# A decoder layer on one core: values masked by ScalarE, four state products per batch on GpSimd, and a new order of the projection units

## What is computed

```
dA = exp(A * dt);  dBu = dt * Bm * hs          # 1024 channels, 16 states, 256 positions
s_l = dA_l * s_(l-1) + dBu_l                   # the scan
y = sum over n of s[n] * Cm[n]                 # "C product", then the sum over the states
v = Wv @ source + bv;  out = (softmax(mask * q.k ...) * mask) @ v    # masked values
scale = max(mean(|w|), eps);  wq = clip(round(w / scale), -1, 1)     # ternary weights
```

## Time and profile before

| | us |
|---|---|
| median of three runs | 3782.39 (3778.49 to 3785.61) |
| the profiled execution | 3785.51 |
| span of its profile | 3783.6 |
| mean granted TensorE clock | 0.94 |
| state-space steps, first scan to last scan | 87.7 to 2087.3 |

### The profile page before, as it was taken

One profiled execution on the slowest core, in us unless ns is written; L12 is line 12 of the kernel. 1 busy time (PEld: TensorE's weight loads), 2 busy tenths in 40 slices (PEclk: granted clock), 3 DMA queues, 4 the chain that ended last, 5 costly groups with the idle time before them and its releaser, 6 DMA issues. The chain is left out here.

```text
span 3783.6 us, 53475 instructions
## 1 busy us (share of the span) xinstructions
PE 3172.5 (84%) x16161; PEld 1878.1 (50%) x16194; DVE 3054.2 (81%) x2990; ACT 2540.9 (67%) x4872; POOL 2143.7 (57%) x1352
## 2 busy tenths in 40 slices
PE   6878888888888888888876478898898899859998
PEld 4666566656665666566655233343343333324444
DVE  1999998989989989899999377777787777638887
ACT  3878787877777877777776035565565556647777
POOL 1888887878888878788888123343243334210000
PEclk9989999999999999999996789999999999989999
DMA  4012101110121012101110445454553544331111
GB/s 151 3 57 70 71 14 58 70 71 12 59 71 71 12 60 70 69 10 63 71 65 1 123 134 153 137 158 134 161 160 114 171 149 128 102 100 42 44 44 37
DMA packets 157518, 311.41 MB, mean 82 GB/s; under 512 B 21969, under 2 KB 77393, under 8 KB 157089
## 3 DMA queue, kind: packets, MB, share of 16 engines
q1 hardware_dynamic: 152880, 299.46, 24.6%
q10 hardware_dynamic: 4352, 8.39, 0.6%
HBM read 216.11 MB, written 91.69 MB: 81 GB/s over the span
## 5 line engine op out<-in xcount | busy, mean ns | idle before, releaser
L681 DVE TENSOR_TENSOR_SCAN states<-states,bu 128x1024 f32<-128x1024 f32 x512 | 1173.7, 2292 | 188.4 <-POOL bu L612 107.2
L612 POOL TENSOR_TENSOR bu<-du,bc 128x1024 f32<-128x1024 f32 x512 | 1196.3, 2361 | 117.1 <-DVE states L681 113.9
L545 ACT ACTIVATE states<-dt,negA 128x256 f32<-128x256 f32 x2048 | 853.1, 464 | 440.6 <-DVE hc L693 380.4
L1162 ACT ACTIVATE pt<-s_ps 128x512 f32<-128x512 f32 x1024 | 573.4, 597 | 427.9 <-PE s_ps L1057 418.7
L1313 DVE TENSOR_REDUCE mmax<-s_ps 128x2 f32<-128x1024 f32 x512 | 624.4, 1223 | 288.0 <-PE s_ps L1048 272.8
L421 PE MATMUL y_ps<-id_sb,hc 128*128 128x128 f32 x4096 | 575.3, 286 | 143.3 <-DVE hc L693 143.2
L693 DVE TENSOR_TENSOR hc<-states,bc 128x1024 f32<-128x1024 f32 x512 | 626.8, 1224 | 52.3 <-DVE states L681 0.9
L421 PEld LDWEIGHTS y_ps<-id_sb,hc 128*128 128x128 f32 x4096 | 490.8, 147 | 308.1 <-DVE hc L693 262.6
L1057 PE MATMUL s_ps<-qst,kst 105*128 105x512 bf16 x1024 | 387.0, 392 | 13.1 <-ACT pt L1162 5.1
L1048 PE MATMUL s_ps<-kst,qst 102*128 102x512 bf16 x1024 | 325.3, 401 | 83.9 <-issue 42.7
L390 PE MATMUL proj<-xpad,diagW 128*128 128x256 f32 x1024 | 260.4, 388 | 42.1 <-ACT xpad L488 42.1
(11 more groups left out here) (153 smaller groups left out, 4529.3 us busy)
## 6 DMA issues: line engine op xcount, KB each, us to landing
bc<-bc_scratch SPq DMA_DIRECT2D x128, 512.0 KB, 4.7
stack_d<-parts SPq DMA_DIRECT2D x192, 256.0 KB, 3.0
w_raw<-in_w_ffn SPq DMA_DIRECT2D x32, 768.0 KB, 6.1
qst<-stack_d SPq DMA_DIRECT2D x64, 384.0 KB
kst<-stack_d SPq DMA_DIRECT2D x64, 384.0 KB
x<-xres SPq DMA_DIRECT2D x32, 512.0 KB, 3.5
xT_sb<-in_xT SPq DMA_DIRECT2D x16, 512.0 KB, 3.5
xres<-in_x SPq DMA_DIRECT2D x16, 512.0 KB, 3.7
```

The source lines that it names most:

```text
L545: a = act.activation(states[:, bank, first:first + SEQ], dt[:, t, :], ACT.Exp, scale=negA[:, t, c * NS + n:c * NS + n + 1])
L612: pool.tensor_tensor(bu[:, buf, :].rearrange("p (n l) -> p n l", n=NS), du[:, t % (2 * GRP):t % (2 * GRP) + 1, :].to_broadcast([P, NS, SEQ ...
L681: m = dve.tensor_tensor_scan(dst, dst, bu[:, BU_OF[k][0], half * 2 * SEQ:(half + n) * 2 * SEQ], 0.0, ALU.mult, ALU.add)
L1162: act.activation(pt[:, g % 2, u % HG, st, :], s2_ps[:, st % 2], ACT.Exp).then_inc(exp_done, 1)
```

## The change

1. **C products.** At steps 0, 12, 20 and 28 of each batch (`POOL_STEPS`) the scan writes to a new SBUF buffer `hp`, and POOL multiplies it by C three steps later (`times_C` of the gpsimd block, after `inputs` of that step). PE adds it to `y_ps` two steps after its own step. The wait of `decays` two steps on is then for the scan, not for the product.
2. **Order of units.** `LONG`, `SHORT`, `LAG`, `CLIP`, `SERIES_AT` and `SKIP_COST` are new. By `plan()` the parts of l begin at step 18 (before 19), g3 ends at step 28 (before 25), d3 is emptied at step 15 (before 19), the two gate functions run at steps 18 and 30 (before 16 and 28), and clip and series come two steps after the logarithm (before one).
3. **Weight measuring.** Three pieces of 512 columns at steps 7, 13 and 21 take the place of one of 1536 at step 22; each has its own DMA. The sums are kept by piece and added by three small matmuls at the end.
4. **Values.** DVE only adds the bias; ACT multiplies by the mask (`mask_values`), after the exponentials of units 12 and 13. PE's first value product of a batch waits for it.
5. **Rounding on POOL.** The two one-operation forms get a second operation that multiplies by 1.0.

```diff
+PART = 512
+W_PARTS = PIECE // PART
...
-LONG = [("s", 0, 1), ("s", 1, 1), ("c", 0, 1), ("c", 1, 1), ("s", 2, 1), ("s", 3, 1), ("c", 2, 1), ("c", 3, 1),
-        ("s", 4, 1), ("s", 5, 1), ("c", 4, 1), ("s", 6, 1), ("c", 5, 1), ("s", 7, 1), ("c", 6, 1), ("c", 7, 1),
-        ("g", 0, 1), ("g", 1, 1), ("g", 2, 1), ("l", 0, 1), ("g", 3, 1), ("o", 0, -1), ("o", 1, -1)]
-SHORT = [(0, "d", 1, 0), (2, "t", 3, -1), (6, "d", 2, 0), (9, "t", 0, 0), (17, "d", 3, 0), (18, "t", 1, 0),
-         (22, "d", 0, 1), (28, "t", 2, 0)]
+LONG = [("s", 0, 1), ("s", 1, 1), ("c", 0, 1), ("c", 1, 1), ("s", 2, 1), ("c", 2, 1), ("s", 3, 1), ("s", 4, 1),
+        ("c", 3, 1), ("s", 5, 1), ("c", 4, 1), ("s", 6, 1), ("g", 0, 1), ("c", 5, 1), ("s", 7, 1), ("c", 6, 1),
+        ("c", 7, 1), ("g", 1, 1), ("l", 0, 1), ("g", 2, 1), ("o", 0, -1), ("g", 3, 1), ("o", 1, -1)]
+SHORT = [(0, "d", 1, 0), (2, "t", 3, -1), (6, "d", 2, 0), (10, "t", 0, 0), (13, "d", 3, 0), (17, "t", 1, 0),
+         (22, "d", 0, 1), (27, "t", 2, 0)]
...
-LAG = {"s": 2, "c": 2, "g": 3, "l": 1, "d": 2, "t": 2, "o": 1}
-SKIP_COST = 0
+LAG = {"s": 2, "c": 2, "g": 2, "l": 2, "d": 2, "t": 1, "o": 1}
+SKIP_COST = 1.5
...
+POOL_STEPS = (0, 12, 20, 28)
+DVE_STEPS = [k for k in range(STEPS) if k not in POOL_STEPS]
+POOL_AT, SUM_AT = 3, 2
...
-CLIP, SERIES_AT, SOFT = 1, 1, 4
-W_AT = 22
+CLIP, SERIES_AT, SOFT = 2, 2, 4
+W_AT = (7, 13, 21)
...
-            def load_piece(b):
-                sp.dma_start(w_raw[:, :], w_ffn[bass.ds(b * P * PIECE, P * PIECE)].rearrange("(p c) -> p c", p=P))\
-                  .then_inc(w_piece_in, 16)
+            def load_piece(b, i):
+                if not (b == 0 and i == 0):
+                    sp.wait_ge(w_piece_done, b * W_PARTS + i)
+                src = w_ffn[bass.ds(b * P * PIECE, P * PIECE)].rearrange("(p c) -> p c", p=P)
+                sp.dma_start(w_raw[:, :], src[:, i * PART:(i + 1) * PART]).then_inc(w_piece_in, 16)
...
-                pe.wait_ge(hc_dve, dve_chunk(b, k) + 1)
-                src = hc[:, k % 2, :]
+                if k in POOL_STEPS:
+                    pe.wait_ge(hc_pool, pool_products(b, k))
+                    src, done = hp.ap(), sum_pool
+                else:
+                    pe.wait_ge(hc_dve, products(b, k))
+                    src, done = hc[:, DVE_STEPS.index(k) % 2, :], sum_dve
...
-                    sum_states(b, k)
+                    if k not in POOL_STEPS:
+                        sum_states(b, k)
+                    if k - SUM_AT in POOL_STEPS:
+                        sum_states(b, k - SUM_AT)
...
-                        act.wait_ge(hc_dve, b * STEPS + before + 1)
+                        if before % STEPS in POOL_STEPS:
+                            act.wait_ge(scan_done, b * STEPS + before + 1)
+                        elif before < 0:
+                            act.wait_ge(hc_dve, products(b - 1, before + STEPS))
+                        else:
+                            act.wait_ge(hc_dve, products(b, before))
...
-                act.wait_ge(w_piece_in, (b + 1) * 16)
-                if not (isinstance(b, int) and b == 0):
+            def measure(b, i):
+
+                act.wait_ge(w_piece_in, (b * W_PARTS + i + 1) * 16)
+                if i == 0 and not (isinstance(b, int) and b == 0):
                     act.wait_ge(w_added, b)
-                for i, cols in enumerate((w_raw[:, 0:GU_COLS], w_raw[:, GU_COLS:])):
-                    a = act.activation(cols, cols, ACT.Abs, accum_out=w_piece[:, i:i + 1])
-                a.then_inc(w_piece_done, 1)
+                act.activation(w_raw[:, :], w_raw[:, :], ACT.Abs, accum_out=w_piece[:, i:i + 1]).then_inc(w_piece_done, 1)
...
+
+            def times_C(b, k):
+                if k == POOL_STEPS[0]:
+                    pool.wait_ge(c_in[k % CPT], (b + 1) * 16)
+                pool.wait_ge(scan_done, b * STEPS + k + 1)
+                pool.tensor_tensor(hp[:, :], hp[:, :], bc[:, k % CPT, 1, :], ALU.mult).then_inc(hc_pool, 1)
...
+                    if k - POOL_AT in POOL_STEPS:
+                        times_C(b, k - POOL_AT)
...
+                if k in POOL_STEPS and not (isinstance(b, int) and b == 0 and k == POOL_STEPS[0]):
+                    dve.wait_ge(sum_pool, pool_products(b, k) - 1)
                 for bank, half, n in runs_of(k):
-                    dst = states[:, bank:bank + n, :].rearrange("p i l -> p (i l)")
-                    m = dve.tensor_tensor_scan(dst, dst, bu[:, BU_OF[k][0], half * 2 * SEQ:(half + n) * 2 * SEQ], 0.0, ALU.mult, ALU.add)
+                    src = states[:, bank:bank + n, :].rearrange("p i l -> p (i l)")
+                    dst = hp[:, half * 2 * SEQ:(half + n) * 2 * SEQ] if k in POOL_STEPS else src
+                    m = dve.tensor_tensor_scan(dst, src, bu[:, BU_OF[k][0], half * 2 * SEQ:(half + n) * 2 * SEQ], 0.0, ALU.mult, ALU.add)
                 m.then_inc(scan_done, 1)
...
+                dve.wait_ge(sum_dve, products(b, t * CPT + CPT - 1))
+                if any(k // CPT == t for k in POOL_STEPS):
+                    dve.wait_ge(sum_pool, pool_products(b, t * CPT + CPT - 1))
                 if not (isinstance(b, int) and b == 0 and t < 2):
...
+                    if g == 0:
+                        pe.wait_ge(v_masked, (b + 1) * PER_BATCH["v"])
...
+            def mask_values(s, par, idx):
+                if idx == 0:
+                    act.wait_ge(vm_in, (s + 1) * 16)
+                act.wait_ge(ev["v"], seq("v", s, idx))
+                for a in range(2):
+                    st = 2 * idx + a
+                    m = act.activation(vaug[:, par, st, :, 0:HDIM], vtmp[:, a, :].rearrange("p (h d) -> p h d", h=HEADS),
+                                       ACT.Identity, scale=vm[:, st:st + 1])
+                m.then_inc(v_masked, 1)
...
                 elif u == 9:
-                    pool.tensor_scalar(w_raw[:, :], w_raw[:, :], MAGIC, None, ALU.add)
+                    pool.tensor_scalar(w_raw[:, :], w_raw[:, :], 1.0, MAGIC, ALU.mult, ALU.add)
                 elif u == 12:
-                    pool.tensor_scalar(w_int[:, :], w_raw[:, :], MAGIC, None, ALU.subtract).then_inc(w_piece_done, 1)
...
                                              ALU.add, ALU.mult).then_inc(ev[kind], 1)
                 elif kind == "v":
-                    if idx == 0:
-                        dve.wait_ge(vm_in, (batch + 1) * 16)
+                    if not (isinstance(batch, int) and batch == 0 and idx == 0):
+                        dve.wait_ge(v_masked, seq("v", batch, idx) - 1)
                     dve.tensor_tensor(vtmp[:, :, :], misc[:, :].rearrange("p (a o) -> p a o", a=2),
-                                      bv_sb[:, :].rearrange("p (a o) -> p a o", a=1).to_broadcast([P, 2, SEQ]), ALU.add)
-                    dve.drain()
-                    for a in range(2):
-                        st = 2 * idx + a
-                        m = dve.tensor_scalar(vaug[:, par, st, :, 0:HDIM], vtmp[:, a, :].rearrange("p (h d) -> p h d", h=HEADS),
-                                              vm[:, st:st + 1], None, ALU.mult)
-                    m.then_inc(ev["v"], 1)
+                                      bv_sb[:, :].rearrange("p (a o) -> p a o", a=1).to_broadcast([P, 2, SEQ]),
+                                      ALU.add).then_inc(ev["v"], 1)
```

More of the change, by code:

```diff
@@ L276, in runs_of, with products, pool_products @@
             return [(lo, 0, 2)] if hi == lo + 1 else [(lo, 0, 1), (hi, 1, 1)]
-        def dve_chunk(b, k):
-            return b * STEPS + k
+        def products(b, k):
+            return b * len(DVE_STEPS) + sum(i <= k for i in DVE_STEPS)
+        def pool_products(b, k):
+            return b * len(POOL_STEPS) + sum(i <= k for i in POOL_STEPS)
         @block.sync
@@ L328, in _ @@
                 f = b + 1
-                if b > 0:
-                    sp.wait_ge(w_piece_done, b)
-                load_piece(b)
+                for i in range(W_PARTS):
+                    load_piece(b, i)
                 if active(f):
@@ L423, in sum_states @@
                                       skip_group_check=True)
-                m.then_inc(sum_dve, 1)
+                m.then_inc(done, 1)
             def front():
@@ L461, in tail @@
                 pe.wait_ge(ev["o"], BATCH * PER["o"])
-                pe.matmul(proj_banks[:, 0, 0:2], ones[:, :], w_sum[:, :], start=True, stop=True).then_inc(w_total, 1)
+                for bank, parts in enumerate((range(GU_COLS // PART), range(GU_COLS // PART, W_PARTS))):
+                    for i in parts:
+                        m = pe.matmul(proj_banks[:, bank, 0:1], ones[:, :], w_sum[:, i:i + 1], start=(i == parts[0]),
+                                      stop=(i == parts[-1]))
+                m.then_inc(w_total, 1)
             over_batches(pe, front, body, tail)
@@ L687, in times_C @@
                     dve.wait_ge(c_in[c], (b + 1) * 16)
-                if not (isinstance(b, int) and b == 0 and k < 2):
```

(10 more changed lines are left out.)

32 lines of the change are left out of this document (19 added, 13 removed).

## The result

The changed kernel takes 3660.95 us (median of 4 runs, 3659.44 to 3663.86), the kernel before 3783.52 in the same measurement: ratio 0.968, 95% interval 0.966 to 0.970. The gain is 123 us. The forecast was 3632, a gain of 151; the result lies in its range and 29 us above it. One of the four executions of experiment 9 took 6310 us and is left out of its time.

A forecast was written before the change was run, and what follows sets the result against it. VectorE's chain (116.4 of 125.2 us a batch) plus waits bounds the state-space stage; in attention, VectorE's masking held by GpSimd's rounding. 3785.5 - 72 - 78 = 3635, less 3.1 for the runs' median: 3632 us, range 3598 to 3690.

The forecast's parts named there:

- State-space stage: A batch of the state-space stage falls from 125.2 to 120.7 us with the loop turn, saving 72 us over 16 batches.
- C products: Four products of 1.14 us leave VectorE's chain each batch; on GpSimd each was taken as 2.32 us.
- GpSimd and ScalarE's waits: State-space stage: GpSimd becomes the fullest engine at 117.5 us a batch; ScalarE's waits fall from 7.5 to 5.3 us.
- the state-space stage gives nothing: Rival (0.11): GpSimd's products, TensorE's order or the late xT put back VectorE's saving; only attention gains, 3704 us.
- Costed at nothing: State-space stage: TensorE's work, late xT and first broadcasts of B, weight pieces and final matmuls cost nothing or under 1 us.
- Values: Attention: masking on ScalarE brings units 12 and 13 from 14.12 to 8.52 us, in 14 batches, saving 78 us.
- The rounding: GpSimd's new rounding forms take between 1.47 and 4.18 us; nobody waits for them, so nothing either way.
- The hold is not VectorE's alone: Rival (0.03): in attention ScalarE's masking waits for GpSimd too, giving 3710 us.
- ScalarE delays the exponentials: Rival (0.12): in attention ScalarE's added 1.64 us a batch lies on the path, 23 us back, giving 3655 us.
- Slower: Rival (0.03): scans writing `hp` to SBUF are held by GpSimd, 3.45 us for each of 64, giving 3853 us.

The follow-up runs named there:

- experiment 9: The changed kernel with the one-operation rounding forms of the kernel before: 3658.1 us (0.966).
- Experiment 8: The changed kernel with the unit order, lags and series steps of the kernel before, the four C products kept on GpSimd: 3759.8 us.
- experiment 2: The kernel before with the two-operation rounding forms alone, masking still on VectorE: 3804.2 us (1.0057).
- experiment 4: The kernel before with the bf16 rounding moved from unit 12 to unit 9, masking still on VectorE: 3734.8 us (0.987).
- experiment 6: The changed kernel with SyncE's loads of stack groups 1 and 2 moved behind the store of x, row maxima and mask row: 3634.2 us (0.961).
- experiment 7: The changed kernel with the loads of stack groups 1 to 3 moved into the next batch: 3636.4 us (0.961).
- experiment 10: The changed kernel with 16 already met waits ahead of TensorE's attention code, so its loop stands 8 instructions further on: 3639.5 us (0.961).
- experiment 12: The kernel before with only the values masked by ScalarE, plus 16 already met waits ahead of TensorE's attention code: 3700.7 us (0.978).
- experiment 5: The changed kernel with all 32 C products on VectorE again, new unit order, lags and weight pieces kept: 3674.7 us.
- experiment 1: The kernel before with the values' masking on ScalarE and nothing else, its rounding forms kept: 3732.2 us (0.986).

## Why the prediction was right, and where it was off

- *State-space stage, 72 us forecast, 66.8 measured.* A batch without a turn was to take 119.4 and takes 119.5. The gap is at the edges: the turns cost 4.7 us (five batches of 124.2) for the 4.25 of the earlier trace rows, and the first batch took 122.2. That the batch came out to 0.1 us is in part luck, since the waits in it were split wrongly.
- *C products.* 2.36 us for the 2.32 taken. VectorE's step is 2.51 with yT, where 3.53 + 0.33 less 1.14 gives 2.72; it is 0.2 shorter.
- *GpSimd and ScalarE's waits.* Rather the wrong way round. GpSimd is the fullest engine as said (93% busy in the stretch, forecast 96), but ScalarE's waits did not go from 7.5 to 5.3: over the whole stage they fell by 5 us of 72, while those for bu doubled. The sum of both was right; the split was not. The 7.5 us before were misread already: by the earlier trace rows the decays held scans for 72.3 us, 4.5 a batch, and bu for 32 after the first scan, 2.0 a batch. The step most worth keeping is one that I costed without knowing its weight: that logarithm, burst and product are spread. Experiment 8 shows that in the old order the products lose 32 us. My rival "the state-space stage gives nothing" had the right mechanism for that order, and the new table is what kept it away. (It was argued with "four engines within 12 us of each other"; three are, and ScalarE is 17.5 below VectorE in the earlier trace rows.)
- *Costed at nothing.* It held: no wait for xT or a first broadcast of B shows up in the stage.
- *Values, 78 us forecast, 61.2 measured.* This is the term that was mis-sized. The 5.6 us for each pair of units is right (14.12 to 8.37, and 85.0 us in all), and the hold is shown to be what cost them (experiments 2 and 4). The step that failed is "saved in each of the 14 batches", taken as the stage's gain: I multiplied the saving and did not ask what was next late at the end of the batch. That gave back 18.8 us behind unit 14 and 5.0 in units 0 to 11. The splits, stores and stack loads are a chain that follows the units; with two units 5.7 us shorter, the turn now begins 0.6 us after the last of three bulk loads is issued in place of 6.3 (TensorE's last matmul and last `kst<-mask_d` before it: 2769.3 and 2768.7 after, 2873.2 and 2866.9 before). Experiments 6, 7 and 10 shorten these turns or take TensorE's unnamed wait away, by 20 to 25 us. They don't show that the full 78 would have been kept: the kernel before has 42.7 us of that wait too, and it was not run with either edit.
- *The rounding*: nothing either way, and so it is (experiment 9). But the forms did not lie between 1.47 and 4.18: the bf16 one takes 5.38, slower than the one-operation form. With VectorE still behind it that would have cost 20 us (experiment 2).
- *Rivals.* "The hold is not VectorE's alone": ScalarE's masking is never over 0.508 us with the rounding beside it. By that rule of the Trainium skill (SBUF — State Buffer, Who interferes with whom) ScalarE never waits for GpSimd; the trace agrees. "ScalarE delays the exponentials": no wait of `pt` for it shows. "Slower" (held `hp` scans, over 2.3 us): the longest is 2.291.

## What to carry to other kernels

When VectorE's odd instruction is ten times its median, look for a GpSimd instruction that ends when it ends; here separating the two by GpSimd's order was worth as much as moving the work. When work is moved to an engine whose other work comes in bursts, the place of the burst can decide the sign: price order and move together. And multiply a saving by the number of rounds only after asking which transfer, issued on a chain of its own, is ready when the shorter round ends.

## What the runs showed of the hardware

- **TensorE's loop may or may not be fetched anew, by where it stands.** The same attention loop cost 45 packets of 16 KB on q8 in one place and none 8 instructions further on. That was worth 19.5 us (experiment 10) and 33 us (experiment 12) of a stage of 1042 to 1075, and 22 in experiment 5 by accident. So an edit that changes TensorE's instruction count in an earlier stage can shift a later one by 20 to 33 us, and the packets of q8 should be compared first. Equal counts don't settle it: experiments 1 and 9 both have 150 packets and the same attention code, and are 11 us apart in that stage. Before and after both have 150 as well, so some 10 us of the change's 61.2 in attention may be placement and not the edit. No other shift was tried, and why one place is fetched anew and the other not stays open.
- **Fetch competes with bulk loads.** With three groups and a store issued just ahead, the last of three packets started 7.7 to 11.7 us after the first at the five turns of the changed kernel; with one group and the store, 4.9 to 6.0 (experiment 6).
- **GpSimd's `tensor_scalar` on 1536 columns**: 1.47 us with two operations and f32 output (4.10 with one), but 5.38 with two and bf16 output (one: 4.17 with VectorE's held masking beside it, 4.09 without, in experiments 1 and 4).
- What stays open: the 8 us a turn that remain with q8 fetching, ScalarE's unnamed wait at the turns, and the waits for group 0 (12 us beside the first one), which no run removed.
